# First attention of a two-layer kernel: q and k kept whole in fp32, the scores of a head pair as two products on the two row halves of the array, one PSUM bank for every projection

## The reference, cut to what matters

```
xn, latn = layernorm(ctx), layernorm(layernorm(x))
q = latn @ Wq                                     # 256 x 1024 for each of 8 batches
k, v = split(concat(xn, latn) @ Wkv)              # 512 x 1024 each
weight = softmax(einsum('bhld,bhnd->bhln', q * scale, k * scale))
out = einsum('bhln,bhnd->bhld', weight, v)
x = x + out.reshape(b, l, INNER) @ Wo
```

## Time and profile before

| | us |
|---|---|
| median of 3 runs (1675.08 to 1678.4) | 1675.24 |
| profiled execution | 1679.34 |
| its span in the trace | 1677.6 |
| PE busy over the span | 1476.6 (88%) |
| DVE, ACT, POOL busy | 1020.5, 879.3, 458.2 |
| first attention in the trace | from 0 to 730 |

### The profile page before, as it was taken

The page is one execution under the profiler, slowest core; times in us unless marked ns, Lnnn a source line. Parts: engine busy times, 40 slices in busy tenths (PEclk is TensorE's granted clock), DMA queues, the critical chain, the costliest instruction groups (busy, mean ns, idle before and its releaser), DMA issues. The chain is left out here.

```text
span 1677.6 us, 28402 instructions
## 1 busy us (share of the span) xinstructions
PE 1476.6 (88%) x9884; PEld 1198.7 (71%) x9884; DVE 1020.5 (61%) x2142; ACT 879.3 (52%) x2200; POOL 458.2 (27%) x395
## 2 busy tenths in 40 slices
PE   3899999999999999959799998499999629999995
PEld 3678777777777778747698896365655518888885
DVE  5877777777777876755321114477778654444452
ACT  2676767675767777735211113366666214445442
POOL 5110101010101010033200015232322015777774
PEclk9999999999999999977899999599999659999998
DMA  3300000000000000012279993100000223445442
GB/s 113 110 14 1 14 1 14 1 14 2 14 1 14 1 1 1 1 38 93 112 253 312 318 329 69 29 14 7 14 1 2 92 78 101 120 120 126 122 115 34
DMA packets 72255, 118.17 MB, mean 70 GB/s; under 512 B 6864, under 2 KB 52944, under 8 KB 72112
## 3 DMA queue, kind: packets, MB, share of 16 engines
q1 hardware_dynamic: 61408, 99.66, 18.0%
q0 software_dynamic: 10704, 16.65, 4.9%
HBM read 97.68 MB, written 18.61 MB: 69 GB/s over the span
## 5 line engine op out<-in xcount | busy, mean ns | idle before, releaser
L435 ACT ACTIVATE a_p<-a_s,a_negmax 128x512 f32<-128x512 f32 x256 | 176.0, 688 | 156.9 <-DVE a_negmax L603 115.3
L603 DVE TENSOR_REDUCE a_negmax<-a_s 128x1 f32<-128x512 f32 x256 | 176.2, 688 | 47.9 <-PE a_s L298 37.9
L207 POOL TENSOR_TENSOR a_o_l<-a_o,a_o_h 128x256 fp32r<-128x256 f32 x64 | 47.0, 735 | 559.7 <-ACT a_o_h L460 559.7
L1491 ACT ACTIVATE h_probs<-h_scores,h_negmax 128x256 f32<-128x256 f32 x256 | 117.8, 473 | 83.4 <-DVE h_negmax L1658 83.4
L307 PEld LDWEIGHTS a_t<-ident,a_p 128*128 128x128 f32 x1024 | 120.6, 140 | 52.9 <-issue 18.1
L307 PE MATMUL a_t<-ident,a_p 128*128 128x128 f32 x1024 | 156.9, 276 | 0.6 <-DVE a_pT L618 0.6
L1903 POOL TENSOR_TENSOR n_w_l<-n_raw,n_w_h 128x768 fp32r<-128x768 f32 x64 | 118.3, 1849 | 75.2 <-ACT n_w_h L1946 75.2
L597 DVE TENSOR_TENSOR a_k_hl<-a_k_p,a_k_hl 64x512 fp32r<-64x512 f32 x128 | 88.2, 689 | 71.3 <-ACT a_k_hl L418 70.2
L325 PE MATMUL a_out_p<-a_pT,a_v 128*64 128x256 f32 x1024 | 124.6, 385 | 0.0
L297 PE MATMUL a_s<-a_k_hl,a_q_hh 128*128 128x512 f32 x256 | 108.2, 423 | 9.1 <-ACT a_p L435 7.1
L1658 DVE TENSOR_REDUCE h_negmax<-h_scores 128x4 f32<-128x1024 f32 x64 | 78.1, 1221 | 49.6 <-PE h_scores L1585 49.6
(11 more groups left out here) (325 smaller groups left out, 4290.2 us busy)
## 6 DMA issues: line engine op xcount, KB each, us to landing
e_w_in<-in_L_ffn_gate_up_proj SPq DMA_DIRECT2D x31, 1024.0 KB
n_raw<-in_L_ffn_w SPq DMA_DIRECT2D x64, 384.0 KB, 3.0
e_w_out<-in_L_ffn_down_proj SPq DMA_DIRECT2D x31, 512.0 KB
rows_in<-a_zeros SPq DMA_DIRECT2D x1, 3968.0 KB, 15.6
e_rows<-rows_in SPq DMA_DIRECT2D x31, 128.0 KB, 5.1
rows_out<-e_result POOLq DMA_DIRECT2D x31, 128.0 KB, 4.6
x<-in_x SPq DMA_DIRECT2D x8, 256.0 KB, 2.9
a_ctx_in<-in_ctx SPq DMA_DIRECT2D x8, 256.0 KB, 3.1
```

What stands on the lines that cost most here:

```text
L435: act.activation(probs[j][:, :], scores[j % 2][:, :], ACT.Exp, bias=negmax[:, j:j + 1], accum_out=total[:, r % 2, j % 2, j // 2:j // 2 + 1 ...
L603: dve.tensor_reduce(negmax[:, j:j + 1], scores[j % 2][:, :], AX.X, ALU.max, negate=True).then_inc(max_set, 1)
L1491: ins = act.activation(probs[s % 4][:, j, :], scores[s % 2][:, j // 2, j % 2, :], ACT.Exp, bias=negmax[:, s % 4, j:j + 1], accum_out=total ...
```

## The change

- q and k are copied out of PSUM whole, in fp32, by one ACT operation each of 128 partitions. The split tiles, `low_q`, `low_k` and the two memsets of POOL go.
- A score half is two plain fp32 products, head 0 on partitions 0 to 63 and head 1 on partitions 64 to 127 of the same tiles, into two banks. The scores take four banks, and `maximum` takes both heads in one operation of 128 x 1024.
- q, k and v share one bank, proj, in the order q, k, v of the next pair's needs: `project_k` waits for the copy of q, `project_v` for that of k, `project_q` for that of v. v is made in the step of its own pair, no longer ahead of it.
- `set_v` goes from ACT to DVE. `turn` has 8 transposes for both heads of a query half. In `attend` the transposes come last.
- `project_out` goes from step 2 to 1, `turn_inputs` from 4 and 5 to 3 and 4, `fill` to the beginning of steps 4 and 5, `set_out` one step later. `prepare` has eight parts in each of steps 0 and 1 and three in step 2.

Of replaced code only some lines are shown; it stands in the excerpt above.

```diff
-k_hl = [[sb(f"a_k_hl{i}{h}", [P, N], F32R) for h in range(2)] for i in range(2)]
-q_hh = [sb(f"a_q_hh{i}", [P, 2, S], F32R) for i in range(2)]
-q_l = [sb(f"a_q_l{i}", [P, 2, S], F32R) for i in range(2)]
+k, q = [sb(f"a_k{i}", [P, N]) for i in range(2)], [sb(f"a_q{i}", [P, S]) for i in range(2)]
 halves = [slice(0, DH), slice(DH, P)]
...
-scores = [psum(f"a_s{i}", [P, N]) for i in range(2)]
+scores = [psum(f"a_s{i}", [P, 2, N]) for i in range(2)]
 turned_p = [psum(f"a_t{i}", [P, NC, P]) for i in range(2)]
-out_p, k_p, v_p = psum("a_out_p", [P, 2, S]), psum("a_k_p", [P, N]), psum("a_v_p", [P, 2, 2 * P])
-q_p = psum("a_q_p", [P, N])
+out_p, proj = psum("a_out_p", [P, 2, S]), psum("a_proj", [P, N])
+v_p = proj[:, :].rearrange("p (c n) -> p c n", c=2)
...
-    for par in range(2):
-        pool.memset(q_l[par][:, :, :].bitcast(F32), 0.0).then_inc(zeroed, 1)
...
+    def project_q(b, r, bp, starting):
         if starting:
             pe.wait_ge(w_ready, r // 2 + 1)
...
+        if r == 0:
+            pe.wait_ge(kvl_set, KC * b + KC)
+        project(proj[:, 0:S], 0, r, bp, slice(S, N)).then_inc(q_done, 1)
+    def project_k(b, r, bp):
+        pe.wait_ge(q_set, PAIRS * b + r + 1)
+        project(proj[:, :], 1, r, bp, slice(0, N)).then_inc(k_done, 1)
...
-        pe.matmul(scores[j % 2][:, :], q_hh[r % 2][:, h, rows], k_hl[r % 2][h][:, :], start=True, stop=False)
-        pe.matmul(scores[j % 2][:, :], q_l[r % 2][:, h, rows], k_hl[r % 2][h][:, :],
...
+    def score(b, r, half):
+        n, at = 2 * (PAIRS * b + r) + half, slice(half * P, (half + 1) * P)
+        if half == 0:
+            pe.wait_ge(q_set, PAIRS * b + r + 1)
+            pe.wait_ge(k_set, PAIRS * b + r + 1)
+        wait(pe, exp_set, n - 1)
+        for h, rows in enumerate(halves):
+            ins = pe.matmul(scores[half][:, h, :], q[r % 2][rows, at], k[r % 2][rows, :], start=True, stop=True)
+        ins.then_inc(s_done, 1)
+    def turn(b, r, half):
+        n = 2 * (PAIRS * b + r) + half
+        pe.wait_ge(exp_set, n + 1)
+        for h, free in enumerate((even_set, odd_set)):
+            wait(pe, free, n)
+            for c in range(NC):
+                ins = pe.transpose(turned_p[h][:, c, :], probs[2 * half + h][:, c * P:(c + 1) * P], g.ident[:, :])
+            ins.then_inc(t_done[h], 1)
...
         wait(pe, o_set, s)
...
         for c in range(NC):
             for h in range(2):
                 at = r % 2 * P + h * DH
                 ins = pe.matmul(out_p[h * DH:(h + 1) * DH, 0, :], v[r // 2 % 2][:, c, at:at + DH],
                                 probsT[r % 2][h][:, c, :], start=(c == 0), stop=(c == NC - 1))
+        pe.wait_ge(spread_set, s + 1)
+        for half in range(2):
+            ins = pe.transpose(out_p[:, 1, half * P:(half + 1) * P], inverses[r % 2][:, half, :, :], g.ident[:, :])
...
             score(b, r, 0)
+            pe.wait_ge(k_set, PAIRS * b + r + 1)
+            if r == 2:
+                wait(pe, added, b)
+            if r in (4, 5) and last < 2:
+                pe.wait_ge(filled, KC * (b + 1) + r - 3)
+            project_v(b, r // 2, r % 2, bp, first and bp == 0)
             if prev:
...
+                turn(*prev, 1)
             if nxt:
...
+                pe.wait_ge(v_set, PAIRS * b + r + 1)
+                project_q(*nxt, first and bp == 0)
             score(b, r, 1)
...
+            turn(b, r, 0)
             if nxt:
...
+                project_k(*nxt)
             if prev:
                 attend(*prev)
...
+            if nxt:
+                if (r == 1 and not first) or (r in (3, 4) and last < 2):
+                    pe.wait_ge(k_set, PAIRS * b + r + 2)
+                if r == 1 and not first:
+                    project_out(b - 1)
+                if r in (3, 4) and last < 2:
+                    turn_inputs(b + 1, r - 3)
...
-    project_k(0, 0, 0, True)
-    project_q(0, 0, 0)
-    project_v(0, 0, 0, 0, True)
-    project_v(0, 0, 1, 0, True)
+    project_q(0, 0, 0, True)
+    project_k(0, 0, 0)
...
+        wait(act, s_done, 2 * s - 2)
+        act.activation(q[r % 2][:, :], proj[:, 0:S], ACT.Copy, scale=QSCALE).then_inc(q_set, 1)
     def set_k(b, r):
...
+        s = PAIRS * b + r
+        act.wait_ge(k_done, s + 1)
+        wait(act, s_done, 2 * s - 2)
+        act.activation(k[r % 2][:, :], proj[:, :], ACT.Copy).then_inc(k_set, 1)
+    def exponent(b, r, half, h):
+        n = 2 * (PAIRS * b + r) + half
+        if h == 0:
+            act.wait_ge(max_set, n + 1)
+            wait(act, t_done[1], n - 1)
+            wait(act, inv_set, PAIRS * b + r - 1)
+        ins = act.activation(probs[2 * half + h][:, :], scores[half][:, h, :], ACT.Exp,
+                             bias=negmax[:, half, h:h + 1], accum_out=total[:, r % 2, half, h:h + 1])
+        if h == 1:
+            ins.then_inc(exp_set, 1)
...
         for r in range(PAIRS):
...
+            prev, nxt, done = before(b, r, first), after(b, r, bp, last), before_that(b, r, first)
+            exponent(b, r, 0, 0)
+            exponent(b, r, 0, 1)
             if prev:
...
+                set_even(*prev, 1)
+                spread(*prev)
+            if nxt:
+                set_q(*nxt[:2])
+            set_even(b, r, 0)
+            if done:
+                high_o(*done)
+            if r in (4, 5) and last < 2:
+                high_kv(b + 1, 1 - bp, r - 4)
+            exponent(b, r, 1, 0)
             if nxt:
                 set_k(*nxt[:2])
...
+            exponent(b, r, 1, 1)
...
+    def set_v(b, group, half):
+        m = PAIRS * b + 2 * group + half
+        dve.wait_ge(v_done, m + 1)
+        wait(dve, o_done, m - half - 2)
+        dve.tensor_copy(v[group % 2][:, 2 * half:2 * half + 2, :], v_p[:, :, :]).then_inc(v_set, 1)
+    def maximum(b, r, half):
+        dve.wait_ge(s_done, 2 * (PAIRS * b + r) + half + 1)
+        dve.tensor_reduce(negmax[:, half, :], scores[half][:, :, :], AX.X, ALU.max, negate=True).then_inc(max_set, 1)
...
+            for part in range(8 * r + 2 * j, 8 * r + 2 * j + 2):
+                if last < 2 and part < PARTS:
+                    prepare(b + 1, part)
         for r in range(PAIRS):
...
+            prev, nxt, done = before(b, r, first), after(b, r, bp, last), before_that(b, r, first)
             if r == 2 and not first:
                 add(b - 1)
             if r in (4, 5) and last < 2:
                 fill(b + 1, r - 4)
+            maximum(b, r, 0)
+            set_v(b, r // 2, r % 2)
+            if prev:
+                set_odd(*prev, 1)
+                invert(*prev)
+            between(r, 0)
+            if done:
+                set_out(*done)
+            between(r, 1)
+            maximum(b, r, 1)
+            set_odd(b, r, 0)
+            between(r, 2)
+            between(r, 3)
...
```

More of the change, by code:

```diff
@@ L225, in step @@
                     for r in range(PAIRS):
[L226 to L231, removed]
+                        done = before_that(b, r, first)
+                        if done:
+                            low_o(*done)
+                        if r in (4, 5) and last < 2:
+                            low_kv(b + 1, 1 - bp, r - 4)
                 pool.memset(g.ident[:, :], 0.0).then_inc(ident_set, 1)
@@ L315, in attend @@
                     pe.wait_ge(v_set, s + 2 - r % 2)
-                    pe.wait_ge(spread_set, s + 1)
                     wait(pe, o_set, s)
-                    for half in range(2):
-                        pe.transpose(out_p[:, 1, half * P:(half + 1) * P], inverses[r % 2][:, half, :, :], g.ident[:, :])
                     for c in range(NC):
@@ L351, in step @@
                         if nxt:
-                            project_k(*nxt, first and bp == 0)
+                            pe.wait_ge(v_set, PAIRS * b + r + 1)
+                            project_q(*nxt, first and bp == 0)
                         score(b, r, 1)
-                        if prev:
-                            turn(*prev, 3)
+                        turn(b, r, 0)
                         if nxt:
-                            if r == 3:
-                                wait(pe, added, b)
-                            if r in (5, 6) and last < 2:
-                                pe.wait_ge(filled, KC * (b + 1) + r - 4)
-                            project_q(*nxt)
@@ L363, in step @@
-                        score(b, r, 2)
-                        turn(b, r, 0)
-                        group = r // 2 + 1
-                        if group < GROUPS:
-                            project_v(b, group, r % 2, bp, first and bp == 0)
-                        elif last < 2:
-                            project_v(b + 1, 0, r % 2, 1 - bp, False)
-                        score(b, r, 3)
+                            project_k(*nxt)
                         if prev:
                             attend(*prev)
-                        turn(b, r, 1)
@@ L374, in step @@
-                        if r == 2 and not first:
-                            pe.wait_ge(ql_set, PAIRS * b + r + 2)
```

(22 more changed lines are left out.)

146 lines of the change are left out of this document (25 added, 121 removed).

## The result

The changed kernel is slower: 1709.53 us in the median of 4 runs (1705.74 to 1715.57), beside 1675.16 for the kernel before on the same chip; the ratio is 1.0208, 95% interval 1.0186 to 1.0229, so +31 to +38 us. Its profiled execution took 1711.26 us with a span of 1709.5, against 1679.34 and 1677.6: +32. (The profile of the kernel before is none of the four runs of this comparison, whose median is 4 us lower.)

What follows compares the result with a forecast made beforehand. PE was taken to bound the first 730 us, its clock at 1.00. Terms 33 - 31 + 13 + 13 + 3 = +31 on the 1675.2 us median gave 1706 us, own range 1692 to 1722, full range 1672 to 1726.

Steps and rivals of the forecast that it cites:

- PE's own work: First attention, PE: only scores and the weight waits after them change, +0.52 us a step, 64 steps, +33 us.
- Waits gone: First attention: PE's waits for copies and subtractions on ACT and DVE all go, -31 us.
- v's copy: Each step, `project_q` waits for DVE's copy of v from the one bank: 0.2 us, 64 times, +13 us.
- k's copy behind the norm: Steps 0 and 1: ACT's k copy, behind second maximum and norm parts, holds PE 0.6 and 1.3 us; +13 us.
- `fill`: Steps 4 and 5 of a batch: `project_v` waits for `fill` on DVE, 0.2 to 0.3 us each, 14 times, +3 us.
- The start: Starting order, two v projections no longer ahead of the first score: taken at nothing, among items within 3 us.
- `turn_inputs`: PE, two of four transposes per batch, 0.8 us; transposes were taken to keep their numbers.
- Rival B: The new waits for v's and k's copies do not come: +2 us, 1677 us; chance 0.17.
- C: Score pair on 64 rows costs only its two passes, 1.72 us a step: 1660 us; chance 0.12.
- D: The two heads' score products do not overlap on PE: +99 less 29 of waits, 1776 us; chance 0.06.

Runs made afterwards that it cites:

- e2: Changed kernel with `project_q` moved behind the second score half on PE; ratio 1.0203 to the kernel before.
- e6: e1 with the two inverse transposes moved ahead of `attend`'s products; ratio 1.0081 to the kernel before.
- v2: Changed kernel with a pair's scores adjacent on PE, both maxima adjacent on DVE, q behind the first `turn`, norm parts spread; ratio 1.0001 to the kernel before.
- e5: Kernel before without DVE's subtractions for the low parts of q and k (zeros instead), PE's products as many; ratio 0.9825 to the kernel before.
- e7: Kernel before with the odd head's last `set_odd` copy moved ahead of `low_k` on DVE; ratio 0.9901 to the kernel before.
- e1: Changed kernel with the norm's 19 parts spread over steps 0 to 3 in DVE's order; median 1688.34 us, ratio 1.0109 to the kernel before.
- e4: Changed kernel with q and k tiles in fp32r, one pass per score, low halves left out; 1656.14 us, ratio 0.9912 to the kernel before.
- e3: Changed kernel with both products of a score half on the same row half, even heads computed twice; 1811.02 us, ratio 1.0827 to the kernel before.

## Why the prediction was right

The forecast was +31 and the whole shows +35 (31 to 38). The mechanism is the one forecast: PE's own work grows, the old waits go, new ones come for v's and k's copies. That the number is so near is in part luck, since by the stage alone, where all of it happens, the forecast was 9.5 us short. The terms, each with what it measured:

- **PE's own work, +33: measured +41.** The step is 0.79 longer, 0.15 of it the wait for v's copy, leaving 0.64 for the 0.52 taken. Its parts were mis-sized in opposite directions. The score pair is 1.06, and I had added 0.09 for the change-over ahead of it, but that falls on q (0.91 for 0.80) only; so I had the scores at +0.37 where they are +0.19. I charged restarts behind the scores alone (0.15), yet every border between tiled products (scores, `attend`) and full ones costs: q in front of a score 0.11, k in front of `attend` 0.11, the second `turn` behind a score 0.06 (0.85 for 0.79 in e2), the inverse transposes in front of a score 0.05. e6 and v2 move such borders and get 0.16 and 0.26 back, so this is shown. A further 0.09 is no border: eight transposes in one go take 0.79 even between two full products (e2), where twice four took 2 x 0.36, one group of them 0.05 more.
- **Waits gone, -31: measured -31.0** by e5, at the attention's end. The equality is luck: e5 gains 5.6 of it at the start, which I had left out, and 22.6 in the six batches where I had 28. What the account missed was the waits' nature: e7 takes away 16 of the 31 with the split still there, so half was to be had without the change.
- **v's copy, 0.2 a step, +13: measured 0.15,** about +10. `turn` goes out in 0.95 where eight transposes take 0.79 (e2), and q's first product starts 0.06 behind the end of the copy, so the walk's mechanism is as described. No variant here takes this wait away and leaves the rest as it is.
- **k's copy behind the norm, 0.6 and 1.3 us, +13: measured 1.06 and 1.12**, 2.2 a batch, +15; without them (e1) 2.33. Place, releaser and sum were right, the division between the two steps was not. For the first step most of the difference is the 0.5 us that L486 stood still beside POOL: without them it would be 0.6 (an estimate, 1.06 - 0.48).
- **`fill`, +3: measured about +3.** In the steps that begin with it v starts 1.26 us behind the score's start instead of 1.06 (448.01 to 449.27), 0.20 in 14 steps.
- **The start, at nothing: +0.3** up to the first POOL instruction (68.00 for 67.68), but of two parts that cancel: an earlier start and some 8 us lost, which e1 gets back.
- **`turn_inputs`, unchanged in the sum: so measured.** They take 0.53 each for 0.36 to 0.40, but the inverse transposes ahead of them 0.09 less, and the 0.07 that they cost the transposes ahead of them before is gone.
- **Left over:** 41 + 10 - 31 + 15 + 3 = 38 of 40.5, and this is kinder than the parts are, because e5's -31.0 has 5.6 at the start where the changed kernel has +0.3. By stretches it reads: in the six batches the terms above make 9.0 us a batch (8 x 0.79, 2.2, 0.4 and 0.1 more for the output projection) and the batch grows by 4.4, so 4.6 of old waits went, 28 in six, as forecast; e5 keeps 0.9 a batch of them, for POOL, which the changed kernel has not. Before and behind the six batches the POOL row stands at different places of its step in the two kernels, so I take the first score of a batch's pair 3: 8.1 us later in batch 1 (161.18 for 153.10), 34.5 in batch 7 (706.52 for 672.04), 40.5 at the end. The last 6.0 are five steps of 0.79 and 2.0 behind them; there PE waits 1.73 us for DVE's `a_o` ahead of the last `attend` (757.92), where the kernel before has shorter waits.

Rival B fell because the waits for k came where the walk had them. C fell on e4 and e3: the second pass costs 0.63 a pair, and its decision point, a pair below 0.9, was missed with 1.06. D fell on e3: without overlap a pair is 1.91, and the kernel at 1811, near the 1776 + 29 of that rival without its credit.

That the whole shows 35 and the stage 40.5 is not explained. The code behind the attention is the same, its length varies by 21 us between profiles, and no experiment ties it to the change. In the two profiles the difference of 8.6 us lies in one place: the first product with `e_hidden` comes 117.6 us behind the attention's end before and 109.0 in the changed kernel (879.04). It comes at 108.3 to 108.7 in e1 to e4, which ran on one chip, and at 118.1 to 119.7 in the other six, which ran on two others; the kernel before, too, has its lower median on the first of these chips. So it may be the chip and not the kernel; the two were not taken apart.

## What to carry to other kernels

Work taken off an engine that is not the bound is worth the waits it caused and no more, and such a wait can sometimes be had more cheaply by changing the order in the queue: here moving one copy ahead of one subtraction gave half of it, for nothing. The products tiled by rows here overlap well (1.06 us for 1.91), but a border with full products cost TensorE 0.05 to 0.11 us each time, so keep tiled work together. Where buffers are merged, walk the queue of the engine that frees them: what stands ahead of the copy sets the price.

## What was not expected of the hardware

Small DVE operations stood still while POOL worked. The changed kernel's start, POOL and then DVE:

```profile
37.73 3.46 POOL L227 TENSOR_TENSOR a_w_l<-a_raw,a_w_h 128x1536 fp32r<-128x1536 f32 x1
41.13 1.04 POOL L225 CAST a_out_h<-a_raw 128x1024 fp32r<-128x1024 f32 x1
42.25 2.35 POOL L227 TENSOR_TENSOR a_out_l<-a_raw,a_out_h 128x1024 fp32r<-128x1024 f32 x1
...
46.78 2.37 POOL L227 TENSOR_TENSOR a_out_l<-a_raw,a_out_h 128x1024 fp32r<-128x1024 f32 x1
```

```profile
38.35 0.74 DVE L511 BATCH_NORM_STATS2 a_stats<-a_ctx_in 128x6 f32<-128x256 f32 x2
39.12 0.38 DVE L515 BATCH_NORM_AGGREGATE a_mv<-a_stats 128x2 f32<-128x6 f32 x4
39.54 1.68 DVE L484 TENSOR_SCALAR a_var<-a_mv 128x4 f32<-128x4 f32 x1
41.25 0.95 DVE L485 TENSOR_SCALAR a_guess<-a_var 128x4 int32<-128x4 int32 x1
42.23 0.17 DVE L486 TENSOR_SCALAR a_guess<-a_guess 128x4 int32<-128x4 int32 x1
42.43 2.18 DVE L492 TENSOR_TENSOR a_tmp<-a_guess 128x4 f32<-128x4 f32 x1
44.65 0.16 DVE L493 TENSOR_TENSOR a_tmp<-a_tmp,a_var 128x4 f32<-128x4 f32 x1
...
46.97 2.20 DVE L492 TENSOR_TENSOR a_tmp<-a_rstd 128x4 f32<-128x4 f32 x1
```

An operation on four columns, 0.16 us elsewhere, takes 0.95 to 2.20 us and ends each time within 0.04 us of the POOL instruction beside it (41.22 and 41.19, 42.20 and 42.17, 44.61 and 44.60, 49.17 and 49.15). Statistics and aggregates in the same stretch keep their length. The Trainium skill, "GPSIMD Engine Reference", section "1. Specifications", has the interfaces to SBUF shared with VectorE, with contention for DVE instructions in a two-port mode or with two inputs in SBUF; L492 has two such inputs, and the trace agrees. L484 and L485 have one and were held too; whether they run in a two-port mode no trace here shows. In the changed kernel those operations stand ahead of the second maximum, so PE's next score comes at 47.47. e1_parts, which has them later, has it at 42.03: 5.4 of the 8 us that its start gains, of which 1.1 is a first score that comes sooner (31.19 for 32.30) and 4.3 is what L484, L485 and the first L492 take above their usual time. The kernel before is held in the same way (its first such operation takes 2.26 us from 42.53, beside POOL's that ends at 44.77), and in the hardware loop the same thing makes 0.5 us of the wait for k's copy.
